# A macaron block with expert-choice routing: search slots, last passes, layer norms and outputs moved between engines

## The reference

```python
x = x + 0.5 * ffn(layernorm(x)); x = x + attn(layernorm(x)); x = x + 0.5 * ffn(layernorm(x))   # x: 4 x 1024 x 128

def ffn(x):                       # 8 experts, each takes the k = S / 8 * 2 = 256 tokens of a batch that like it best
    affinity = softmax(x @ gate_w.T)                    # over the experts
    gating, idx = top_k(affinity.transpose(0, 2, 1), k)
    h = silu(x[idx] @ w_gate.T) * (x[idx] @ w_up.T)     # 128 -> 512
    return zeros.at[idx].add(gating * (h @ w_down.T))   # 512 -> 128

def attn(x):                      # 16 heads of 8, rotary angles over three axes, 1024 x 1024 scores per head
    q, k, v = rope(x @ Wq + bq), rope(x @ Wk + bk), x @ Wv + bv
    return softmax(q @ k.T * 8 ** -0.5) @ v @ Wo + bo
```

## Time and profile before

| | us |
|---|---|
| median of 3 runs | 1288.36 |
| the runs | 1285.54 to 1290.73 |
| the profiled execution | 1295.63 |
| its span, first to last instruction | 1293.5 |
| TensorE matmuls busy | 1107.3 |
| VectorE busy | 1005.9 |
| ScalarE busy | 768.8 |
| GpSimd busy | 458.1 |

### The profile page before, as it was taken

One profiled execution on the slowest core, in us unless ns is written; L12 is line 12 of the kernel. 1 busy time (PEld: TensorE's weight loads), 2 busy tenths in 40 slices (PEclk: granted clock), 3 DMA queues, 4 the chain that ended last, 5 costly groups with the idle time before them and its releaser, 6 DMA issues.

```text
span 1293.5 us, 25046 instructions
## 1 busy us (share of the span) xinstructions
PE 1107.3 (86%) x9424; PEld 474.9 (37%) x9424; DVE 1005.9 (78%) x2058; ACT 768.8 (59%) x1433; POOL 458.1 (35%) x434
## 2 busy tenths in 40 slices
PE   3159799799489899999999999989999879898993
PEld 3127566466132122222222222212323246565652
DVE  3665975575788899999999999999897676875541
ACT  2033122432157899999997999889688944122220
POOL 2033777565647331100010000103011036667875
PEclk9999999899678899999999999999999988999997
DMA  8012445437713131112110112101210215344452
GB/s 267 11 55 69 85 89 106 96 81 192 186 53 96 27 89 41 39 40 59 33 43 25 44 53 75 41 6 55 71 32 12 51 29 131 76 94 103 90 112 25
DMA packets 92560, 93.19 MB, mean 72 GB/s; under 512 B 14556, under 2 KB 69852, under 8 KB 92408
## 3 DMA queue, kind: packets, MB, share of 16 engines
q1 hardware_dynamic: 69912, 74.80, 20.1%
q0 software_dynamic: 22528, 16.79, 9.2%
HBM read 63.32 MB, written 30.06 MB: 72 GB/s over the span
## 4 chain that ended last, share of the span: by engine, by line
PE 39%; DVE 29%; issue 13%; ACT 8%; POOL 5%; DMA 3%; SPq 2%; another core or an unknown queue 0%; DVEq 0%; POOLq 0%; ACTq 0%
DVE mx L1606 17%; PE pO L1233 6%; ACT Pt L941 6%; PE pA L1124 6%; PE pS L1113 5%; PE pS L1254 4%; PE pA L1169 3%; DVE ge L1323 3%; PE pS L1114 3%; POOL out_dram L578 3%; PE pO L1114 2%; POOL xg L560 2%; PE pS L1032 2%; DVE onehot L1404 1%; PE pA L1004 1%
## 5 line engine op out<-in xcount | busy, mean ns | idle before, releaser
L1606 DVE TENSOR_REDUCE mx<-pA 128x2 f32<-128x1024 f32 x512 | 587.1, 1215 | 30.0 <-PE pA L1169 29.1
L941 ACT ACTIVATE Pt<-pS 128x512 f32<-128x512 f32 x1024 | 556.2, 596 | 56.1 <-PE pS L1254 50.5
L1233 PE MATMUL pO<-Pt,Vst 128*16 128x256 f32 x4096 | 325.8, 391 | 11.4 <-ACT U L932 11.4
L842 ACT ACTIVATE Pt<-pS 128x512 f32<-128x512 f32 x128 | 76.2, 597 | 244.2 <-PE pS L1113 217.4
L560 POOL DMA_INDIRECT xg<-zd,idx x128 | 126.1, 985 | 209.6 <-DVE idx L1419 125.5
L1169 PE MATMUL pA<-Kst,Qst 48*128 48x512 bf16 x704 | 142.4, 401 | 28.3 <-DVE mx L1606 26.5
L1113 PE MATMUL pS<-Pt,wg 128*128 128x512 f32 x256 | 144.3, 647 | 25.5 <-DVE Pt L1438 13.8
L626 POOL TENSOR_TENSOR mparts<-mx,onesm 128x32 bf16<-128x32 f32 x16 | 4.1, 253 | 445.3 <-DVE mx L1611 445.2
L1254 PE MATMUL pS<-Qst,Kst 51*128 51x512 bf16 x704 | 140.7, 396 | 11.9 <-ACT Pt L941 7.7
L1233 PEld LDWEIGHTS pO<-Pt,Vst 128*16 128x16 f32 x4096 | 68.3, 94 | 206.5 <-issue 115.2
L1124 PEld LDWEIGHTS pA<-wd,Pt 128*128 128x128 f32 x1024 | 120.9, 192 | 20.4 <-issue 15.3
(11 more groups left out here) (188 smaller groups left out, 1076.8 us busy)
## 6 DMA issues: line engine op xcount, KB each, us to landing
wg<-w_gate_dram SPq DMA_DIRECT2D x32, 256.0 KB
wu<-w_up_dram SPq DMA_DIRECT2D x32, 256.0 KB
wd<-w_down_dram SPq DMA_DIRECT2D x32, 256.0 KB
qk<-parts SPq DMA_DIRECT2D x64, 96.0 KB
Kst<-qk SPq DMA_DIRECT2D x132, 32.0 KB
zd<-Z SPq DMA_DIRECT2D x8, 512.0 KB
vp<-pair SPq DMA_DIRECT2D x4, 1024.0 KB
Vst<-vp SPq DMA_DIRECT2D x16, 256.0 KB
```

Source lines behind the costliest of these rows:

```text
L941: S.activation(Pt[:, s % 4, j, r * 512:(r + 1) * 512], pS[:, bank_of(k, 4 * s + 2 * j + r), :], ACT.Exp, scale=SCALE).then_inc(s_exp, 1)
L1233: last = M.matmul(pO[32 * h:32 * h + 16, cols], Vst[k][:, s % 8, h, :], Pt[:, s % 4, h // 2, (h % 2) * 512 + 256 * a:(h % 2) * 512 + 256 * ...
L1606: V.reduce_max(mx2[:, k, 2 * j:2 * j + 2, c, half], pA[ring[q, a] % 2][:, :, :], AX.X).then_inc(s_Ar, 1)
```

## The change

- `place`: search 1 starts one slot later, at (1, 0), and ends at (6, 0). The transposes of the attention's set-up go from pass 10 to pass 11, and the 20 pieces behind them from four a pass to five a pass, (12, 0) to (15, 4). In the second FFN the projection of batch 3 goes to (16, 4) and (17, 0), and search 3 runs five slots a pass, (17, 4) to (21, 4). Pass 22 loses its special order.
- `late`: search 2 begins at tile 20 and ends at 52, the projection of batch 2 goes behind it, to 54 and 63. `compact(16)` and `compact(17)` go to tiles 57 and 61, the token turn of pass 16 between the last value products, and ScalarE's copy ahead of the last result.
- The last `down` of each FFN writes four banks, chunk by chunk (`last_down`); VectorE scales each bank as it is ready (`last_outputs`), and the scatter waits call by call. All scatters wait for each batch's earlier scatter only ahead of that batch's calls.
- Layer norms run by four tiles, at other places; `moments(4)` and `moments(5)` go from (9, 2) to (10, 0) and (10, 2); `deviation(10)` goes to pass 17.
- The outputs of passes 0 to 5 and 16 to 21 are scaled by ScalarE.
- Search steps 5 and 6 use `transpose` instead of a matmul with the identity.
- TensorE waits for the last result only ahead of `gate_up(16, 1)`.

```diff
+SEARCH = (0, 1, 2, 3, 4, 5, 16, 17, 18, 19, 20, 21)
...
     for n in range(NF):
-        place[divmod(3 + n, 4)] = ("f", 1, n)
+        place[divmod(4 + n, 4)] = ("f", 1, n)
     place[8, 0] = ("s", 0)
-    for m in range(1, 5):
-        place[10, m] = ("s", m)
+    place[11, 0], place[11, 1], place[11, 3], place[11, 4] = [("s", m) for m in range(1, 5)]
     for m in range(5, 25):
-        place[divmod(39 + m, 4)] = ("s", m)
-    place[16, 2], place[16, 3] = ("f", 3, 0), ("f", 3, 1)
-    place[17, 0], place[17, 1] = ("p", 3, 0), ("p", 3, 1)
-    for n in range(2, NF):
-        place[divmod(70 + n, 4)] = ("f", 3, n)
+        place[divmod(55 + m, 5)] = ("s", m)
+    place[16, 4], place[17, 0] = ("p", 3, 0), ("p", 3, 1)
+    for n in range(NF):
+        place[divmod(89 + n, 5)] = ("f", 3, n)
...
-    for i, key in enumerate([("p", 2, 0), ("p", 2, 1)] + [("f", 2, n) for n in range(5, NF)]):
-        late[32 * (NQ - 2) + 20 + 2 * i] = key
+    for n, at in zip(range(5, NF), (20, 21, 23) + tuple(range(26, 47, 2)) + (49, 52)):
+        late[32 * (NQ - 2) + at] = ("f", 2, n)
+    late[32 * (NQ - 2) + 54] = ("p", 2, 0)
+    late[32 * (NQ - 2) + 63] = ("p", 2, 1)
...
+        last_bank = [pY, pT, pI, sidebank]
...
-                pool.wait_ge(s_ye, j + 1)
-                for b in batches(j):
-                    if j >= RUN and j % E == 0:
-                        pool.wait_ge(s_out[b], 16)
-                    if adds_before(j):
-                        pool.wait_ge(s_scat[b], adds_before(j))
-                pool.sem_inc(s_held, 1)
                 for k in range(HB * SH):
+                    b = batches(j)[k // SH]
+                    if k % SH == 0:
+                        if j >= RUN and j % E == 0:
+                            pool.wait_ge(s_out[b], 16)
+                        if adds_before(j):
+                            pool.wait_ge(s_scat[b], adds_before(j))
+                    if j % RUN == RUN - 1:
+                        pool.wait_ge(*((s_scaled, 3 * (j // RUN) + k + 1) if k < 3 else (s_ye, j + 1)))
+                    elif k == 0:
+                        pool.wait_ge(s_ye, j + 1)
+                    pool.sem_inc(s_held, 1)
...
+            def outputs(j):
+                act.wait_ge(s_down, j + 1)
+                if j % RUN >= 2:
+                    for b in batches(j - 2):
+                        act.wait_ge(s_scat[b], adds_before(j - 2) + 32)
+                for k in range(HB * SH):
+                    last = S.activation(ye[j % 2][:, k, :], pY[:, k * D:(k + 1) * D], ACT.Copy, scale=gain[j % 6][:, k:k + 1])
+                last.then_inc(s_ye, 1)
...
                     if u == 1:
                         between(it, 1)
+                        if it - 1 in SEARCH:
+                            outputs(it - 1)
                         between(it, 2)
...
+            act.wait_ge(s_pv, 16 * NQ + 1)
+            turn_tokens(RUN)
             result(NQ - 1, 1)
-            deviation(10)
-            act.wait_ge(s_sd, 11)
+            act.wait_ge(s_sd, 10)
             S.activation(warm[:, :], sd[:, 0:8], ACT.Silu)
-            turn_tokens(RUN)
...
+            def last_down(j):
+                p = j % 2
+                pe.wait_ge(s_ye, j)
+                pe.wait_ge(s_xt, j + 1)
+                pe.wait_ge(s_idx, j + 1)
+                pe.wait_ge(*was_read(("s", 24) if j < RUN else ("f", 3, NF - 1)))
+                for i in range(IC):
+                    pe.wait_ge(s_hid, 4 * j + i + 1)
+                    for k in range(4):
+                        last = M.matmul(last_bank[k][:, 0:D], hid[p][:, i, k * P:(k + 1) * P], wd[p][:, i, :],
+                                        start=(i == 0), stop=(i == IC - 1))
+                        if i == IC - 1:
+                            last.then_inc(s_part if k < 3 else s_down, 1)
...
+            def last_outputs(j):
+                for b in batches(j - 2):
+                    dve.wait_ge(s_scat[b], adds_before(j - 2) + 32)
+                for k in range(HB * SH):
+                    dve.wait_ge(*((s_part, 3 * (j // RUN) + k + 1) if k < 3 else (s_down, j + 1)))
+                    V.tensor_scalar(ye[j % 2][:, k, :], last_bank[k][:, 0:D], gain[j % 6][:, k:k + 1], None,
+                                    ALU.mult).then_inc(s_scaled if k < 3 else s_ye, 1)
...
             for at in sorted(late):
-                use(late[at])
-                if late[at] == ("p", 2, 1):
-                    moments(10)
-            first_experts(RUN)
+                if late[at][0] == "f":
+                    use(late[at])
+            all_onehots(RUN)
+            pick(RUN)
+            use(("p", 2, 0))
+            all_onehots(RUN + 1)
+            pick(RUN + 1)
+            use(("p", 2, 1))
+            moments(10)
+            all_onehots(RUN + 2)
```

More of the change, by code:

```diff
@@ L263, in program @@
         s_ye = sem("ye")
+        s_part = sem("part")
+        s_scaled = sem("scaled")
         s_scat = [sem(f"scat{b}") for b in range(B)]
@@ L720, in _ @@
             for it in range(RUN, NIT):
-                if it + 2 < NIT and it != 22:
+                if it + 2 < NIT:
                     gather(it + 2)
@@ L725, in _ @@
                     scatter(it - 1)
-                if it == 22:
-                    gather(it + 2)
                 if it == 19:
@@ L740, in deviation, with normalise @@
                 S.activation(sd[:, tiles(i)], veps[:, tiles(i)], ACT.Sqrt).then_inc(s_sd, 1)
-            def normalise(i, first=0):
+            def normalise(i, first=0, end=CH):
                 act.wait_ge(s_shift, i + 1)
-                if i >= 2:
+                if i >= 2 and not first:
                     act.wait_ge(*turned(i - 2))
@@ L747, in normalise @@
                         act.wait_ge(s_zst, 32 * min(i // 2, 3))
-                for n in range(first, CH):
+                for n in range(first, end):
                     r = i % B * CH + n
@@ L752, in normalise @@
                         last.then_inc(s_zlo, 1)
-                last.then_inc(s_zhi, 1)
+                if end == CH:
+                    last.then_inc(s_zhi, 1)
             def front(hh, n):
@@ L1008, in front @@
                     for k in range(4):
-                        last = M.matmul(bank[:, k * P:(k + 1) * P], aff[:, 4 * (n - 5) + k, :, :].rearrange("p j r -> p (j r)"),
-                                        ident[:, :], start=True, stop=True)
+                        last = M.transpose(bank[:, k * P:(k + 1) * P], aff[:, 4 * (n - 5) + k, :, :].rearrange("p j r -> p (j r)"),
+                                           ident[:, :])
                 elif n == 7:
@@ L1132, in expert @@
                 between(it, 0)
+                if it == RUN:
+                    pe.wait_ge(s_U, 2 * NQ + 1)
                 gate_up(it, 1)
@@ L1138, in expert @@
                     down(it - 1, (2, 3))
-                if it % RUN < RUN - 2 and it != 22:
+                if it % RUN < RUN - 2:
                     compact(it + 2)
@@ L1548, in expert @@
                 between(it, 1)
-                if not first:
+                if not first and it - 1 not in SEARCH:
                     outputs(it - 1)
-                if it + 2 < end and it != 22:
+                if it + 2 < end:
                     pick(it + 2)
@@ L1555, in expert @@
                 between(it, 2)
-                if it == 22:
-                    all_onehots(24)
                 hidden(it, 2)
-                if quarters and it != 22:
+                if quarters:
                     onehots(it + 3, 1)
                 between(it, 3)
-                if it == 5:
-                    all_onehots(8)
                 hidden(it, 3)
-                if it == 22:
-                    pick(24)
-                    onehots(25, 0)
-                    onehots(25, 1)
                 if quarters:
@@ L1600, in _ @@
                 expert(it)
-            outputs(RUN - 1)
+            last_outputs(RUN - 1)
             def piece(q, a):
```

86 lines of the change are left out of this document (51 added, 35 removed).

## The result

Timed in turn with the kernel before, the changed kernel takes 1269.79 us (median of 4 runs, 1264.54 to 1270.77) against 1289.55 (4 runs): ratio 0.9844, 95% interval 0.9807 to 0.988. A second timing, in a later group of runs, gave 1268.77 against 1289.7, 0.9832 (0.9817 to 0.9846). The forecast was 1266, the range 1255 to 1283. The total came out near the forecast, in part by luck: of the eight terms, C came with the wrong sign, and B and D gave more than their bounds allow; the misses cancel.

What follows compares the result with a forecast made beforehand. Limits differ by pass: TensorE's 12.34 us floor in plain passes with GpSimd close behind, VectorE in pure search, GpSimd in the tail. Terms A to H sum to 22.4 us off 1288.4, forecasting 1266 us, range 1255 to 1283.

Steps and rivals of the forecast that it cites:

- C: Passes 9 to 15: moved moments shorten passes 9 and 10, 3.4 us lost again in 11 to 15; -3.6 us.
- B: First eight passes: normalisations by four tiles, outputs on ScalarE, transposes, +0.5 for moved logits; -5.2 us, bounds -2 and -8.
- D: Attention: only the transposes shorten TensorE; -1.0 us (0 to -2).
- A: First search: eight transposing matmuls in f(0,5) and f(0,6) become transposes; -1.9 us.
- H: Last pass and tail: GpSimd's scatters stop waiting for the landing of the one before; -4.7 us (bounds -2 and -7.7).
- F: Passes 19 to 23: five search slots a pass, outputs off VectorE, passes 22 and 23 plain; -6.0 us, bounds -2 and -10.
- E: Attention's end and passes 16 to 18: SiLU 0 some 3 us earlier, then given back; 0, bounds -5 and +4.
- G: Passes 24 to 30: already at the floors of TensorE and GpSimd; 0 (-2 to +3).
- (1): Stalls return elsewhere: weights behind x, GpSimd and later transposes leave little of C and F, half of B; 1275 us, chance 0.25.
- (2): Passes reach TensorE's floor, weights come in time; C, F and H give 9.7 us more: 1256 us, chance 0.10.
- (3): GpSimd pays 0.30 us more per scatter call: +14 us, with returning stalls 1289, no change; chance 0.09.
- (4): TensorE's clock stays at half through passes 17 to 21, waiting for VectorE: 32 us more, 1298 us, chance 0.06.

Runs made afterwards that it cites:

- run 10: Changed kernel with the layer norms of set 2 and 3 again in one block of eight tiles each: 1274.52 us, ratio 0.9875.
- run 3: Kernel before, with only the scaled outputs of passes 0 to 5 and 16 to 21 moved from VectorE to ScalarE: 1290.59 us, ratio 0.9987.
- run 2: Kernel before, with only the searches' eight products with the identity made transposes: 1289.93 us, ratio 0.9986.
- run 1: Kernel before, with only the scatter's wait made per batch instead of for both batches ahead of the first call: 1282.32 us, ratio 0.9921.
- run 4: Changed kernel with the weights of expert 10 issued ahead of the two loads of x1: 1268.42 us, ratio 0.9822.
- run 8: Changed kernel with expert 10's weights ahead of the x1 loads, and scale and shift of set 4 and 5 at (10, 3): 1264.38 us, ratio 0.9776.
- run 6: Changed kernel with the old last pass of each half (one bank, one wait of GpSimd for all four scaled outputs): 1275.9 us, ratio 0.9871.
- Run 7: Changed kernel with the attention's end as before (token turn behind the last values, last result and SiLU table ahead of the copy): 1278.72 us, ratio 0.9891.
- Run 12: The edits of run 8 on the changed kernel, plus the last group's first result loads issued ahead of write_out(2): 1257.79 us, ratio 0.9742.
- run 5: Changed kernel with the scatter's joint wait for both batches put back: 1283.05 us, ratio 0.993.

## Why the prediction was right in the sum and wrong in parts

The forecast of 22.4 us less came as 19.8 by the medians. That the sum fits is partly luck: B and C together were forecast as -8.8 and came as -6.3, B 6 us better and C 9 us worse; and of D's surplus 3 us are the long profile of before. A and H were right in size and mechanism, F in direction.

**A** was right to 0.1: the two uses take 1.09 and 1.11 us, as forecast.

**B**, forecast -5.2, came as -11.5 and -10.0, beyond its bound of -8. The term of pass 0 was mis-sized: I let the blocks of four win 2.5; undoing them costs 3.6 there and 1.0 in pass 1 (run 10). Passes 3 and 4 gave 1.2 and 1.3 for the outputs' 1.1 each: right, and run 3 shows them alone. The transposes' -1.0 is not shown (run 2). And what I booked as a cost, +0.5 for the logits at (2, 0), looks like a gain: in the kernel before and in runs 1 to 3 VectorE's maxima came 2.5 to 3.3 us after the last product in pass 1; in all ten profiles with the new place they came 0.04 after, and passes 1 and 2 fell by 3.4. No run moves this place alone, so the cause of the 3.4 is argued and not shown. Passes 5 to 8, to which I gave nothing, fell by 1.8 and 0.5 in the two profiles.

**C**, forecast -3.6, came as +5.2 and +3.9: the step that failed is "Pass 9 becomes 15.9 (-4.0), pass 10 about 14.0 (-2.4)". They came as +0.4 and +1.9. The mechanism was named (the weights of expert 10, behind the loads of x, are late next), but the wait left was put at 3.5 us, and it was 7.35. By its own times it is 3.7: the last weights issued 11.9 after the first SiLU of pass 9, plus 4.0, against TensorE ready at 12.2. Three of these were off. TensorE was ready 10.9 after that SiLU (1.3); so it was before, for the row gives 234.23 - 6.97 = 227.26 and not the 228.6 that I used. The last weights were issued 12.8 after it (0.9), since SyncE's loads wait for scatter 7, whose calls on GpSimd follow at 0.30 and came later relative to the pass. And TensorE started 5.4 after that issue, not 4.0 (1.4). The trace of before would have told: the last update of these weights' semaphore is at 233.2 there, only 1.0 ahead of TensorE's restart, so moving the moments alone could win at most 1.0 of the 6.97 us. Run 4, which takes only this order away, gives 6.8 in pass 9, the clock at full with it. Pass 10 had a second wait that I left out: scale and shift at (10, 4) behind hidden 3, 3.2 us on TensorE; moving them (run 8) took 0.9 from passes 10 and 11. The give-back of 3.4 in passes 11 to 15 came (+3.5 in 11 to 14). So did the -0.6 from pass 15 to the maxima, but not by the four banks: without them (run 6) it is -1.1.

**D**, forecast -1.0, came as -4.8 and -7.1. Three of it lie in before's own profile: the stretch was 700.6 in run 1, whose attention is the same. For the rest the runs give no cause; the stretch was 696.4 to 700.8 in the ten profiles of the changed kernel and its variants.

**E**, forecast 0, came as -4.0, within its bounds of -5 and +4. Run 7 puts about 3 of it on the order at the attention's end, which I had sized at 3 and then given back: 2 for SyncE's row and 1 for the transposes. Run 12 speaks against the first: with SyncE's order mended the time stayed. In the four other profiles on the two other chips that keep the new order (runs 4, 5, 6 and 8), E was 59.4 to 61.0, as long as the 59.8 before, and the clock was at half for 6.8 or 10.2 us from the logits of pass 18 on. So the gain of E is there in some executions only.

**F**, forecast -6.0, came as -4.0. I had 58.2 for passes 19 to 22 and 12.6 for pass 23 (forecast 14.8, 16.7, 14.0, 12.7, 12.6; measured 15.9, 17.2, 13.8, 13.1, 12.8). The gain is all pass 23, 18.25 before; passes 19 to 22 grew from 58.6 to 60.0, so the five slots a pass gave nothing. For pass 19 I counted four slots, and (19, 0) to (19, 4) hold five. The cause for pass 23 was not what I wrote alone: the gather stands behind a scatter that waits for a landing, and the scatter's edit (run 1) removes that as the new order does (run 5).

**G** +0.9: small. **H**, forecast -4.7, came as -4.4, by the step named: the landings' waits are gone, GpSimd waits 3.1 us for the outputs of pass 30 instead. Run 1 gives 3.8 of it by the wait alone, run 6 0.5 by the banks. In the kernel before the wait per batch is worth 10 us (run 1), and I had priced it at less than 5, since I saw it in the tail only; in the changed kernel 3.6 of it are shown in the tail and none in pass 23 (run 5).

The rivals: (1) has "weights behind x" right, and its total 5 us too slow. (2) is out: C and F came smaller than forecast and not larger. (3) is out: the seven plain passes took 87.2 us against 86.3, 0.1 each, and GpSimd's calls with a wait ahead of each follow at 0.30. (4) is out: PEclk was 0.98 in passes 17 and 18 and 1.00 in 19 to 23.

The Trainium skill ("TensorE: Matmul & The Clock Gate", Terms) gives transpose mode as "4× faster for FP32". The prediction weighed it in A; the measured 1.09 to 1.11 against 2.04 us says 1.8 times against the matmul with the identity, and the term came as the rows gave it.

## What to carry to other kernels

Cut the trace at a fixed event of each pass and give each edit its own stretch; a total that fits can hide a term of the wrong sign. When a wait is taken away and the next late thing is a transfer issued at the same place, look up when that transfer lands: if it is just ahead of the restart (here 1.0 us), almost nothing is won. Its producer (here GpSimd) doesn't speed up with the pass either; better, move the transfer ahead of the load that waits (run 4: 6.8 us from one pass). And ask of every joint wait on a queue that feeds others whether its first call needs all of it: in the kernel before one such wait cost 10 us. What an edit is worth hangs on what else is changed: of these 10 us the new order took a part by itself.

## What the runs showed of the hardware

- Behind the 32 products of 128 x 8 of a search's logits, VectorE's first instruction starts 0.04 to 1.0 us after the last record in most places, but 2.5 to 3.3 us after in four cases of pass 1 (before, runs 1 to 3) and 2.4 to 2.5 us after in three of pass 18 (runs 5, 6, 8), where the records take the same 3.64 us together. In the three of pass 18, 6.8 or 10.2 us at 1.2 GHz begin within 5 us of the last record. Whether the products or the release are late, the profiles don't show.
- Code that is the same in every variant takes 18.2 to 22.0 us in pass 18, and 5.8 to 8.2 us from the last exponential to pass 16 in the new order. The four profiles with 7.8 to 8.2 each have 3.4 us at half clock around the attention's last exponential, the five with 5.8 to 6.1 have none there. Three chips ran the variants, and on one of them (runs 5, 6 and 8) both times are long in every profile. With 3 to 10 us between stretches of the same code, a term under 3 us needs two profiles.
- Two edits on one chain don't add up: outputs by ScalarE are worth 1.7 us of median (within its interval of nothing) in the kernel before, and 4.2 in the changed kernel, where the joint wait is gone and the search has other slots.
